# First attention: the transposes of a unit in two groups instead of four, with their splits behind one another

## The chip, the cores and the metric

The kernel runs on one core of a Trainium2 chip. The metric is the device time of one execution in microseconds (us), lower is better; it is measured as a median over runs. The core's engines work side by side and meet by semaphores: TensorE (PE in the profile, its weight loads PEld), VectorE (DVE), ScalarE (ACT), GpSimd (POOL) and SyncE (SP), which issues the transfers.

## The reference, cut to what matters

The whole program is a network of two layers, each with an attention and a block of experts. The change is in the attention of the first layer:

```python
hidden_states = concatenate([context, latents], axis=1)
q = (latents @ Wq)          # 4 batches, 256 queries, 32 heads of 128
k = (hidden_states @ Wk)    # 1857 keys, 4 key heads, each for 8 heads
v = (hidden_states @ Wv)
scores = einsum('bqhgd,bkhd->bhgqk', q, k) / sqrt(128)
attn = softmax(scores, axis=-1)
out = einsum('bhgqk,bkhd->bqhgd', attn, v)
```

Everything is float32. The kernel multiplies in a faster 32-bit form (fp32r) three times, with every operand split into a high part and a low rest: high by high, high by low, low by high.

## The kernel before, in words

`grouped_attention_block` (line 489) works through 128 units, one for each batch and head. A unit has 256 queries, as two blocks j of 128, and 1857 keys. Its work on each engine:

- **Scores** (`scores`, lines 726 to 739), on TensorE: for each j two halves of the keys. Half 0 is 1024 keys (six matmuls of 512 columns), half 1 is 833 (three of 512 columns, three of 322). They go into four PSUM banks `ps_s`, two for a half. The same four banks serve j = 0, j = 1 and the next unit, so each half waits until the exponential that read the half before it is done.
- **Maximum and negation** (`maximum`, line 872, `negate_maximum`, line 879), on VectorE: one maximum for each half as soon as it is there, then the negated maximum of both.
- **Exponentials** (`exponentials`, line 827), on ScalarE: one for each half, from PSUM into `probs` in SBUF, with the sum read out behind it (a row of its own, ACTIVATION_READ_ACCUMULATOR). Half 0 waits for the negated maximum.
- The first 1024 keys of the probabilities are turned by transfers (`trade`) and by VectorE (`turn_traded`, line 898), split by ScalarE (`turned_high`, line 836) and GpSimd (line 707), and multiplied by the values (`weigh_turned`, four groups of six matmuls).
- The other 833 keys, seven blocks, are turned by **TensorE transposes** (`turn_plain`, line 752) in four groups e = 0 to 3: four transposes each for e = 0, 1, 2 and two for e = 3. The groups go into the two banks of `ps_x` by turns (e even, e odd). `plain_high` on ScalarE (line 845) copies the high part out of the bank, `plain_low` on VectorE (line 908) takes the rest, and after it the bank is free for the group after the next. `weigh_plain` multiplies by the values: six matmuls for e = 0, 1, 2, three for e = 3.
- `take_output` (line 917) copies the unit's 256 columns out; SyncE stores them.

The three matmuls of a product stand in the helper `three` (lines 722 to 724), so a matmul's line in the profile does not tell which group it is; its tiles and its shape do.

Each engine runs its instructions in the order in which its own `step` issues them, written out by hand; a wait holds up all that stands behind it on that engine. A step of TensorE mixes four units: v (scores), w, l and z (one, two and three units further back). Batch 0 is unrolled (32 steps), the other three batches run in a loop whose body has 32 steps, and a few steps follow to drain. In the loop the semaphore counts are register values.

Short names used below: S00, S01, S10, S11 are the scores of block j and half; E00 to E11 their exponentials; m00 to m11 their maxima; T0 to T3 the groups of transposes e; ph0 to ph3 and pl0 to pl3 their high and low splits; z, l in front of T or P the groups of `weigh_turned` and `weigh_plain` of units z and l (zT2, lP0). The order on TensorE before:

zT2, zP2, T1, zP3, S00, T2, S01, zT3, T3, lT0, lP0, lT1, S10, T0, S11, lP1

On ScalarE: E10, ph1, E11, turned_high 0 and 1, ph2, E00, ph3, E01, turned_high 2 and 3, ph0. On VectorE: pl1, turn_traded 1, m00, m01, negation, turn_traded 2, take_output, pl2, turn_traded 3, m10, pl3, m11, negation, pl0, turn_traded 0.

The waits that matter: S00 needs E10 of the unit before done, S01 its E11; S10 needs E00 and S11 E01 of its own unit. ph e needs T e done; pl e needs ph e. T2 needs pl0, T3 needs pl1, T0 of the next unit needs pl2.

Of the kernel before, what the change touches and what calls it, by code (L numbers as in the profile page):

```python
# [488 lines left out]
def grouped_attention_block(nc, held, x, ctx_in, wq, wk, wv, wo, x_res, xn, stats, ident, ones):  # L489
# [40 lines left out]
    with ExitStack() as ctx:  # L530
# [16 lines left out]
        with ExitStack() as stack:  # L547
# [64 lines left out]
            def wait(engine, done, count):  # L612

                if not isinstance(count, int) or count > 0:
                    engine.wait_ge(done, count)
# [104 lines left out]
            def _(pe):  # L720
# [73 lines left out]
                def step(b, r):  # L794
                    v, w, l, z = Unit(b, r - 1), Unit(b, r - 2), Unit(b, r - 3), Unit(b, r - 4)
                    weigh_turned(z, 2)
                    weigh_plain(z, 2)
                    turn_plain(l, 1)
                    weigh_plain(z, 3)
                    scores(v, 0, 0)  # L800
                    turn_plain(l, 2)
                    scores(v, 0, 1)
                    weigh_turned(z, 3, last=True)
                    turn_plain(l, 3)
                    weigh_turned(l, 0, first=True)
                    weigh_plain(l, 0)
                    weigh_turned(l, 1)
                    scores(v, 1, 0)
                    turn_plain(w, 0)
                    scores(v, 1, 1)  # L810
                    weigh_plain(l, 1)
                    if isinstance(b, int) and b * HEADS + r == UNITS + 1:
                        turn_sums()

                run(pe, step, 4)

            @block.scalar
            def _(act):
                def exponentials(u, j, half):
                    if not u.live:  # L820
                        return
                    act.wait_ge(neg_max_done, QT * u.n + j + 1)
                    if half == 0:
                        wait(act, trade_done[j][u.a], TRADE * u.use)
                        wait(act, x_ps, PPAIRS * (u.n - 1))
                    lo, hi = HALVES[half]
                    act.activation(probs[j][u.a][:, lo:hi], s_flat[:, lo:hi], ACT.Exp, bias=neg_max[:, j:j + 1], scale=SCALE,  # L827
                                   accum_out=half_sum[:, bass.ds(QT * u.n + j, 1), half]).then_inc(probs_done, 1)

                def turned_high(u, p):  # L830
                    if not u.live:
                        return
                    q, slot = TPAIRS * u.n + p, (TPAIRS * u.r + p) % RING
                    act.wait_ge(turn_done, q + 1)
                    wait(act, tv_ps, q + 1 - RING)
                    act.activation(t_hi[:, slot, :, :], turned[:, slot, :, :], ACT.Copy).then_inc(t_hi_done, 1)  # L836

                def plain_high(u, e):
                    if not u.live:
                        return  # L840
                    q, slot, bank = PPAIRS * u.n + e, (PPAIRS * u.r + e) % PRING, (PPAIRS * u.r + e) % XBANKS
                    m, rows = len(pair_tiles(e)), plain_rows(2 * e)
                    act.wait_ge(x_ps, q + 1)
                    wait(act, xv_ps, q + 1 - PRING)
                    act.activation(x_hi[0:rows, slot, 0:m, :], ps_x[0:rows, bank, 0:TOK * m].rearrange("p (m n) -> p m n", m=m), ACT.Copy  # L845
                                   ).then_inc(x_hi_done, 1)

                def step(b, r):
                    u, v, w = Unit(b, r), Unit(b, r - 1), Unit(b, r - 2)
                    exponentials(v, 1, 0)  # L850
                    plain_high(w, 1)
                    exponentials(v, 1, 1)
                    turned_high(w, 0)
                    turned_high(w, 1)
                    plain_high(w, 2)
                    exponentials(u, 0, 0)
                    plain_high(w, 3)
                    exponentials(u, 0, 1)
                    turned_high(w, 2)
                    turned_high(w, 3)  # L860
                    plain_high(v, 0)

                run(act, step, 4)

            @block.vector
            def _(dve):
                def maximum(u, j, half):
                    if not u.live:
                        return
                    lo, hi = HALVES[half]  # L870
                    dve.wait_ge(s_ps, 4 * u.n + 2 * j + half + 1)
                    dve.reduce_max(half_max[:, half:half + 1], s_flat[:, lo:hi], AX.X).then_inc(max_done, 1)  # L872

                def negate_maximum(u, j):
                    if not u.live:
                        return
                    dve.wait_ge(max_done, 4 * u.n + 2 * j + 2)
                    wait(dve, probs_done, 4 * u.n + 2 * j - 2)
                    dve.tensor_scalar(neg_max[:, j:j + 1], half_max[:, 0:1], half_max[:, 1:2], -SCALE, ALU.max,  # L879
                                      ALU.mult).then_inc(neg_max_done, 1)  # L880

                def sums():
                    dve.wait_ge(probs_done, 4 * UNITS)
                    dve.tensor_tensor(row_sum[:, :], half_sum[:, :, 0], half_sum[:, :, 1], ALU.add).then_inc(sum_done, 1)

                def inverse_sums():
                    dve.wait_ge(sum_ps, 1)
                    dve.reciprocal(row_inv[:, :], ps_s[:, 0, 0:UNITS * QT]).then_inc(inv_done, 1)

                def turn_traded(u, p):  # L890
                    if not u.live:
                        return
                    q, slot = TPAIRS * u.n + p, (TPAIRS * u.r + p) % RING
                    if p == 0:
                        for j in range(QT):
                            dve.wait_ge(trade_done[j][u.a], TRADE * (u.use + 1))
                    wait(dve, t_done, q + 1 - RING)
                    dve.transpose(turned[:, slot, :, :].rearrange("p k (q r) -> p k q r", r=SQ),  # L898
                                  traded[:, u.a, :, :, 2 * SQ * p:2 * SQ * (p + 1)].rearrange("p j g (k r) -> p k (j g) r", k=2)
                                  ).then_inc(turn_done, 1)  # L900

                def plain_low(u, e):
                    if not u.live:
                        return
                    q, slot, bank = PPAIRS * u.n + e, (PPAIRS * u.r + e) % PRING, (PPAIRS * u.r + e) % XBANKS
                    m, rows = len(pair_tiles(e)), plain_rows(2 * e)
                    dve.wait_ge(x_hi_done, q + 1)
                    dve.tensor_tensor(x_lo[0:rows, slot, 0:m, :], ps_x[0:rows, bank, 0:TOK * m].rearrange("p (m n) -> p m n", m=m),  # L908
                                      x_hi[0:rows, slot, 0:m, :].bitcast(F32), ALU.subtract).then_inc(x_done, 1)

                def take_output(u):
                    if not u.live:
                        return
                    dve.wait_ge(tv_ps, TPAIRS * (u.n + 1))
                    dve.wait_ge(xv_ps, PPAIRS * (u.n + 1))
                    wait(dve, o_stored[u.a], 16 * u.use)
                    dve.tensor_copy(o_part[:, u.a, :], ps_o[:, u.a, 0:TOK]).then_inc(copy_done, 1)

                def step(b, r):
                    v, w, l, z = Unit(b, r - 1), Unit(b, r - 2), Unit(b, r - 3), Unit(b, r - 4)  # L920
                    plain_low(l, 1)
                    turn_traded(l, 1)
                    maximum(v, 0, 0)
                    maximum(v, 0, 1)
                    negate_maximum(v, 0)
                    turn_traded(l, 2)
                    take_output(z)
                    plain_low(l, 2)
                    turn_traded(l, 3)
                    maximum(v, 1, 0)  # L930
                    plain_low(l, 3)
                    maximum(v, 1, 1)
                    negate_maximum(v, 1)
                    plain_low(w, 0)
                    turn_traded(w, 0)
                    if isinstance(b, int) and b * HEADS + r == UNITS + 1:
                        sums()
                        inverse_sums()

                run(dve, step, 4)  # L940
# [1669 lines left out]
```

## Time and profile before

| | us |
|---|---|
| median of 3 runs | 3225.57 (3225.3 to 3226.3) |
| the profiled execution's own time | 3227.55 |
| its span, first to last instruction | 3225.8 |
| TensorE busy | 3023.2 (94%) |
| VectorE busy | 2093.0 (65%) |
| ScalarE busy | 1738.8 (54%) |
| GpSimd busy | 963.1 (30%) |

The profile is of one execution. A timeline row gives the start and length of an instruction (or of several of one kind in a row, with their count), its engine and line, and what it writes and reads; in brackets stands how long the engine was idle before it and what ended that. TensorE's matmuls are pipelined: the next starts before the length of the last is over, so the distance between starts is what one costs. Busy time counts the modelled lengths.

### The profile page before, as it was taken

Reading aid. Unit: us, or ns where it says so; the run is one execution under the profiler, and the core shown is the slowest. Engines: PE = TensorE matmul, PEld = TensorE weight load, DVE = VectorE, ACT = ScalarE, POOL = GpSimd, SP = SyncE. Lnnn points to the kernel's source line nnn. Section 1 sums busy time; section 2 is a strip of 40 time slices with the busy share of each in tenths; the row PEclk is TensorE's granted clock in tenths of the full one; section 3 lists DMA queues with packets and bytes.
Section 4 is the critical chain, followed back from the end, with each engine's and each line's share of the span. In section 5 each row is a group of like instructions: output and inputs, shape, how many; then the busy total and the mean of one; then the engine's idle time right before and its main releaser. Section 6 shows DMA issues by size and latency. Waiting matters only on the chain. (4 is left out here: it accounts for less than half of the span.)

```text
span 3225.8 us, 53851 instructions
## 1 busy us (share of the span) xinstructions
PE 3023.2 (94%) x18414; PEld 2684.3 (83%) x18414; DVE 2093.0 (65%) x3215; ACT 1738.8 (54%) x3297; POOL 963.1 (30%) x773
## 2 busy tenths in 40 slices
PE   8999998999999999999999999979889798898974
PEld 8888886899999999899998999968668788786763
DVE  4333343788888888788887888844444477665575
ACT  3323343676666666666666666632344455553263
POOL 0000121344444444444443444422100124430144
PEclk9999999999999999999999999999899799998997
DMA  7665685766767776677776676567475211101387
GB/s 250 219 217 193 218 284 191 152 161 162 162 157 161 161 161 158 157 158 162 157 160 156 157 164 152 120 189 241 138 277 166 86 29 41 41 28 33 111 294 250
DMA packets 395364, 522.17 MB, mean 162 GB/s; under 512 B 35356, under 2 KB 292684, under 8 KB 395112
## 3 DMA queue, kind: packets, MB, share of 16 engines
q1 hardware_dynamic: 392552, 510.57, 57.9%
q0 software_dynamic: 2560, 8.39, 0.8%
q8 instruction: 140, 2.29, 0.3%
q14 instruction: 112, 0.92, 0.1%
HBM read 238.15 MB, written 146.46 MB: 119 GB/s over the span
## 5 line engine op out<-in xcount | busy, mean ns | idle before, releaser
L707 POOL TENSOR_TENSOR a_t_lo<-a_turned,a_t_hi 128x512 fp32r<-128x512 f32 x512 | 649.4, 1290 | 939.5 <-ACT a_t_hi L836 939.5
L827 ACT ACTIVATE a_probs<-a_ps_s,a_neg_max 128x1024 f32<-128x1024 f32 (+1 forms) x512 | 529.6, 1034 | 475.3 <-DVE a_neg_max L879 472.5
L872 DVE TENSOR_REDUCE a_half_max<-a_ps_s 128x1 f32<-128x1024 f32 (+1 forms) x512 | 571.1, 1115 | 189.4 <-PE a_ps_s L724 185.2
L722 PE MATMUL a_ps_s<-a_k_buf,a_q_buf 128*128 128x512 f32 (+1 forms) x1024 | 419.9, 410 | 17.9 <-ACT a_probs L827 11.6
L723 PE MATMUL a_ps_s<-a_k_buf,a_q_buf 128*128 128x512 f32 (+1 forms) x1024 | 386.0, 377 | 0.0
L724 PE MATMUL a_ps_s<-a_k_buf,a_q_buf 128*128 128x512 f32 (+1 forms) x1024 | 385.2, 376 | 0.0
L908 DVE TENSOR_TENSOR a_x_lo<-a_ps_x,a_x_hi 128x512 fp32r<-128x512 f32 (+1 forms) x512 | 314.4, 614 | 107.4 <-ACT a_x_hi L845 107.4
L454 DVE TENSOR_TENSOR p_out<-p_ps_j,p_out 128x512 fp32r<-128x512 f32 (+3 forms) x196 | 152.9, 780 | 326.9 <-ACT p_out L383 326.9
L898 DVE STREAM_TRANSPOSE a_turned<-xn 128x512 f32<-128x512 f32 x512 | 357.7, 699 | 1.5 <-POOL a_t_lo L707 1.5
L383 ACT ACTIVATE p_out<-p_ps_j 128x512 fp32r<-128x512 f32 (+3 forms) x196 | 142.1, 725 | 339.5 <-PE p_ps_j L288 339.5
L722 PE MATMUL a_ps_o<-a_t_hi,a_v_buf 128*128 128x256 f32 x1024 | 298.9, 292 | 6.3 <-issue 3.8
L836 ACT ACTIVATE a_t_hi<-a_turned 128x512 fp32r<-128x512 f32 x512 | 298.4, 629 | 2.0 <-DVE a_turned L898 2.0
L845 ACT ACTIVATE a_x_hi<-a_ps_x 128x512 fp32r<-128x512 f32 (+1 forms) x512 | 274.5, 537 | 24.6 <-PE a_ps_x L752 13.0
L723 PE MATMUL a_ps_o<-a_t_lo,a_v_buf 128*128 128x256 f32 x1024 | 287.4, 281 | 0.0
L724 PE MATMUL a_ps_o<-a_t_hi,a_v_buf 128*128 128x256 f32 x1024 | 287.3, 281 | 0.0
L752 PE MATMUL a_ps_x<-a_turn,a_probs 128*128 128x128 f32 (+1 forms) x1792 | 279.1, 272 | 0.0
L722 PE MATMUL a_ps_o<-a_x_hi,a_v_buf 128*128 128x256 f32 (+1 forms) x896 | 262.3, 293 | 0.0
L724 PE MATMUL a_ps_o<-a_x_hi,a_v_buf 128*128 128x256 f32 (+1 forms) x896 | 251.6, 281 | 0.0
L723 PE MATMUL a_ps_o<-a_x_lo,a_v_buf 128*128 128x256 f32 (+1 forms) x896 | 251.3, 281 | 0.0
L752 PEld LDWEIGHTS a_ps_x<-a_turn,a_probs 128*128 128x128 f32 (+1 forms) x1792 | 219.0, 140 | 34.9 <-issue 0.2
L722 PEld LDWEIGHTS a_ps_s<-a_k_buf,a_q_buf 128*128 128x128 f32 x1024 | 195.0, 190 | 49.2 <-issue 11.7
L724 PEld LDWEIGHTS a_ps_s<-a_k_buf,a_q_buf 128*128 128x128 f32 x1024 | 194.5, 190 | 34.2
(373 smaller groups left out, 7094.6 us busy)
## 6 DMA issues: line engine op xcount, KB each, us to landing
xn<-a_probs SPq DMA_DIRECT2D x1024, 128.0 KB, 3.4
a_q_all<-p_out SPq DMA_DIRECT2D x64, 512.0 KB
a_q_buf<-a_q_all SPq DMA_DIRECT2D x128, 256.0 KB, 3.3
a_k_buf<-a_k_all SPq DMA_DIRECT2D x64, 464.5 KB, 4.0
a_v_all<-p_out SPq DMA_DIRECT2D x56, 512.0 KB
d_w_raw<-e_wt_all SPq DMA_DIRECT2D x31, 768.0 KB, 6.2
a_k_all<-p_out SPq DMA_DIRECT2D x48, 384.0 KB
a_v_buf<-a_v_all SPq DMA_DIRECT2D x64, 256.0 KB
```

The costliest lines, as they stand in the source:

```text
L454: dve.tensor_tensor(job_views(n, 1)[0], ps, hi.bitcast(F32), ALU.subtract).then_inc(job_done, 1)
L707: pool.tensor_tensor(t_lo[:, slot, :, :], turned[:, slot, :, :], t_hi[:, slot, :, :].bitcast(F32), ALU.subtract).then_inc(t_done, 1)
L722: pe.matmul(o, w_hi, m_hi, start=first, stop=False)
L723: pe.matmul(o, w_hi, m_lo, start=False, stop=False)
L724: return pe.matmul(o, w_lo, m_hi, start=False, stop=last)
L752: tr = pe.transpose(ps_x[0:rows, bank, col:col + P], probs[j][u.a][:, c0:c0 + rows], turn[:, :])
L827: act.activation(probs[j][u.a][:, lo:hi], s_flat[:, lo:hi], ACT.Exp, bias=neg_max[:, j:j + 1], scale=SCALE, accum_out=half_sum[:, bass.ds( ...
L836: act.activation(t_hi[:, slot, :, :], turned[:, slot, :, :], ACT.Copy).then_inc(t_hi_done, 1)
L845: act.activation(x_hi[0:rows, slot, 0:m, :], ps_x[0:rows, bank, 0:TOK * m].rearrange("p (m n) -> p m n", m=m), ACT.Copy).then_inc(x_hi_don ...
L872: dve.reduce_max(half_max[:, half:half + 1], s_flat[:, lo:hi], AX.X).then_inc(max_done, 1)
L898: dve.transpose(turned[:, slot, :, :].rearrange("p k (q r) -> p k q r", r=SQ), traded[:, u.a, :, :, 2 * SQ * p:2 * SQ * (p + 1)].rearrange ...
L908: dve.tensor_tensor(x_lo[0:rows, slot, 0:m, :], ps_x[0:rows, bank, 0:TOK * m].rearrange("p (m n) -> p m n", m=m), x_hi[0:rows, slot, 0:m, ...
```

## The change

Only the order in which three engines issue their instructions is changed. On TensorE T2 moves from between S00 and S01 to directly behind T1, and T0 (of the unit after) from between S10 and S11 to directly behind T3: the four groups of transposes of a step become two, T1 with T2 and T3 with T0. On ScalarE ph2 moves ahead of E11, directly behind ph1, and ph0 ahead of turned_high 2 and 3. On VectorE pl2 moves directly behind pl1. SyncE and GpSimd keep their order; no instruction is added, removed or resized.

```diff
--- before.py
+++ after.py
@@ -796,17 +796,17 @@
                     weigh_turned(z, 2)
                     weigh_plain(z, 2)
                     turn_plain(l, 1)
+                    turn_plain(l, 2)
                     weigh_plain(z, 3)
                     scores(v, 0, 0)
-                    turn_plain(l, 2)
                     scores(v, 0, 1)
                     weigh_turned(z, 3, last=True)
                     turn_plain(l, 3)
+                    turn_plain(w, 0)
                     weigh_turned(l, 0, first=True)
                     weigh_plain(l, 0)
                     weigh_turned(l, 1)
                     scores(v, 1, 0)
-                    turn_plain(w, 0)
                     scores(v, 1, 1)
                     weigh_plain(l, 1)
                     if isinstance(b, int) and b * HEADS + r == UNITS + 1:
@@ -849,16 +849,16 @@
                     u, v, w = Unit(b, r), Unit(b, r - 1), Unit(b, r - 2)
                     exponentials(v, 1, 0)
                     plain_high(w, 1)
+                    plain_high(w, 2)
                     exponentials(v, 1, 1)
                     turned_high(w, 0)
                     turned_high(w, 1)
-                    plain_high(w, 2)
                     exponentials(u, 0, 0)
                     plain_high(w, 3)
                     exponentials(u, 0, 1)
+                    plain_high(v, 0)
                     turned_high(w, 2)
                     turned_high(w, 3)
-                    plain_high(v, 0)
 
                 run(act, step, 4)
 
@@ -919,13 +919,13 @@
                 def step(b, r):
                     v, w, l, z = Unit(b, r - 1), Unit(b, r - 2), Unit(b, r - 3), Unit(b, r - 4)
                     plain_low(l, 1)
+                    plain_low(l, 2)
                     turn_traded(l, 1)
                     maximum(v, 0, 0)
                     maximum(v, 0, 1)
                     negate_maximum(v, 0)
                     turn_traded(l, 2)
                     take_output(z)
-                    plain_low(l, 2)
                     turn_traded(l, 3)
                     maximum(v, 1, 0)
                     plain_low(l, 3)
```

## Rows read from the trace of the kernel before

**Rows 1.** The page, part 1: TensorE, busy us (share of the span) and instructions
```profile
PE 3023.2 (94%) x18414; PEld 2684.3 (83%) x18414; DVE 2093.0 (65%) x3215; ACT 1738.8 (54%) x3297; POOL 963.1 (30%) x773
```

**Rows 2.** Busy time by stretch: us, then each engine's busy us (instructions), clock, DMA
```profile
540.00:560.00 20.00, 10.53 (x28) 8.09 (x29) 5.37 (x7) 5.57 (x9) 0.00 (x0) 0.71 0.32 88
600.00:929.00 329.00, 329.00 (x2289) 304.58 (x2288) 270.08 (x414) 229.32 (x440) 140.36 (x112) 1.00 0.72 161
929.00:1290.00 361.00, 360.92 (x2476) 332.34 (x2476) 292.30 (x448) 248.84 (x478) 150.11 (x119) 1.00 0.71 160
1290.00:1340.00 50.00, 47.41 (x328) 43.47 (x327) 38.60 (x60) 31.88 (x62) 20.31 (x16) 1.00 0.65 154
```

**Rows 3.** Timeline of TensorE, one unit: start, length, engine, line, operation, tiles, count
```profile
1013.97 0.28 PE L722 MATMUL a_ps_o<-a_t_hi,a_v_buf 128*128 128x256 f32 x1
...
1015.38 0.60 PE L752 MATMUL a_ps_x<-a_turn,a_probs 128*128 128x128 f32 x4
...
1016.46 0.40 PE L723 MATMUL a_ps_s<-a_k_buf,a_q_buf 128*128 128x512 f32 x1
...
1017.64 0.60 PE L752 MATMUL a_ps_x<-a_turn,a_probs 128*128 128x128 f32 x4
1018.00 0.48 PE L722 MATMUL a_ps_s<-a_k_buf,a_q_buf 128*128 128x512 f32 x1
1018.31 0.40 PE L723 MATMUL a_ps_s<-a_k_buf,a_q_buf 128*128 128x512 f32 x1
...
1019.24 0.28 PE L722 MATMUL a_ps_o<-a_t_hi,a_v_buf 128*128 128x256 f32 x1
...
1019.96 0.38 PE L752 MATMUL a_ps_x<-a_turn,a_probs 128*65 128x128 f32 x2
...
1020.30 0.28 PE L723 MATMUL a_ps_o<-a_t_lo,a_v_buf 128*128 128x256 f32 x1
...
1022.60 0.39 PE L723 MATMUL a_ps_s<-a_k_buf,a_q_buf 128*128 128x512 f32 x1
```

**Rows 4.** Timeline of ScalarE, the same unit; in brackets idle time and its releaser
```profile
1014.87 1.12 ACT L827 ACTIVATE a_probs<-a_ps_s,a_neg_max 128x1024 f32<-128x1024 f32 x1 [1.88 <-DVE a_neg_max L879]
1015.88 0.19 ACT L827 ACTIVATION_READ_ACCUMULATOR a_probs<-a_ps_s,a_neg_max  x1
1016.09 0.60 ACT L845 ACTIVATE a_x_hi<-a_ps_x 128x512 fp32r<-128x512 f32 x1
1016.59 0.95 ACT L827 ACTIVATE a_probs<-a_ps_s,a_neg_max 128x833 f32<-128x833 f32 x1
1017.42 0.20 ACT L827 ACTIVATION_READ_ACCUMULATOR a_probs<-a_ps_s,a_neg_max  x1
...
1021.00 1.12 ACT L827 ACTIVATE a_probs<-a_ps_s,a_neg_max 128x1024 f32<-128x1024 f32 x1 [1.82 <-DVE a_neg_max L879]
...
1022.11 0.37 ACT L845 ACTIVATE a_x_hi<-a_ps_x 65x256 fp32r<-65x256 f32 x1
...
1026.95 1.12 ACT L827 ACTIVATE a_probs<-a_ps_s,a_neg_max 128x1024 f32<-128x1024 f32 x1 [1.88 <-DVE a_neg_max L879]
```

**Rows 5.** Timeline of VectorE, the same unit
```profile
1014.66 0.68 DVE L908 TENSOR_TENSOR a_x_lo<-a_ps_x,a_x_hi 128x512 fp32r<-128x512 f32 x1
...
1023.96 1.23 DVE L872 TENSOR_REDUCE a_half_max<-a_ps_s 128x1 f32<-128x1024 f32 x1 [0.67 <-PE a_ps_s L724]
1025.10 0.41 DVE L908 TENSOR_TENSOR a_x_lo<-a_ps_x,a_x_hi 65x256 fp32r<-65x256 f32 x1
1025.55 1.02 DVE L872 TENSOR_REDUCE a_half_max<-a_ps_s 128x1 f32<-128x833 f32 x1
1026.61 0.21 DVE L879 TENSOR_SCALAR a_neg_max<-a_half_max 128x1 f32<-128x1 f32 x1
```

**Rows 6.** Timeline in the unrolled batch: VectorE negation and ScalarE exponential behind it
```profile
702.69 0.21 DVE L879 TENSOR_SCALAR a_neg_max<-a_half_max 128x1 f32<-128x1 f32 x1
...
702.94 1.12 ACT L827 ACTIVATE a_probs<-a_ps_s,a_neg_max 128x1024 f32<-128x1024 f32 x1 [1.84 <-DVE a_neg_max L879]
```

## The prediction, made before the changed kernel was run

> **What bounds the kernel now.** I read four views in this order: the busy shares of the page, busy time by stretch, the timelines of TensorE, ScalarE and VectorE over one unit, and the same link in the unrolled first batch. The page says TensorE is busy 94% of the span [rows 1]. By stretch it is busy for all of 600 to 929 us and of 929 to 1290 us [rows 2]; but a matmul's length in this profile is modelled, so a full row does not show that nothing waits. Count units instead. A unit has 83 matmuls (24 of scores, 24 of weigh_turned, 21 of weigh_plain, 14 transposes). So 2289 matmuls in 329 us are 27.6 units of 11.93 us, and 2476 in 361 us are 29.8 units of 12.10 us [rows 2]. The first stretch is the unrolled batch 0, the second the loop over the other batches. In the loop 0.17 us a unit go somewhere.
>
> The timeline shows where [rows 3]. Score matmuls of 512 columns follow each other every 0.235 us (1016.46 to 1017.64 for five). The first of a group is best placed by the second minus 0.235: S00 really starts at 1016.225 (1016.46 less 0.235), S01 at 1018.075, S10 at 1022.365. On ScalarE, E10 runs from 1014.87 to the end of its read-out at 1016.07, and S00 starts 0.155 later [rows 3, 4]. E00 starts at 21.00; with the same 1.20 + 0.155 it frees S10 at 1022.36, which is when S10 starts. So in the loop both first halves of the scores start when the exponential that frees their banks lets them. S01 is different: E11 ends at 1017.62, could free S01 at 1017.78, and S01 starts at 1018.075, with 0.30 us to spare. That spare is there because T2 stands between S00 and S01.
>
> **TensorE: fewer borders between transposes and matmuls.** Nothing is added or removed; 14 transposes stay 14. T2 starts at 1017.64 and the second matmul of S01 at 1018.31: 0.67, less 0.235 for the first matmul, is 0.435 for four transposes and one border. T3 starts at 1019.96 and the second matmul of lT0 at 1020.30: 0.34, less 0.12 for one of six matmuls that take 0.705 (zT2 and zP2 take 1.41), is 0.22 for two transposes and one border. From the two, a transpose takes 0.108 and a border 0.005. That the first matmul behind T2 shows 0.31 to the next (1018.00 to 1018.31) instead of 0.235 is then the last transpose, not a border. Bounds for each border taken away: 0, and 0.08 if that excess were a border after all; for 2 x 125 borders at most 20 us, and only where TensorE is the bound. I take 0, as the two equations leave nothing.
>
> What the order does is move 0.435 of work from between the score halves to in front of the first ones: S00 and S10 get 0.435 more time for E10 and E00. That removes the loop's waits there, worth at most 12.10 - 11.93 = 0.17 a unit. But S01 now follows S00 after 6 x 0.235 = 1.41 instead of 1.85.
>
> **VectorE: S11 is no longer what its maximum waits for.** m10 started at 1023.96, pl3 at 1025.10, m11 at 1025.55 [rows 5]. m11 there waited for S11: it starts 0.04 after pl3's end, where a VectorE instruction that need not wait overlaps the one ahead. With T0 gone from between, S11 is ready 0.435 earlier, but m11 still stands behind m10 (1.14) and pl3. pl3 lasts 0.41; the overlap is 0.08 (m10 lasts 1.23 and pl3 starts after 1.14), so I take 0.33, with 0.45 (the distance seen) as the upper end. m11 then starts 1.47 after m10 instead of 1.59; measured against S11's end that is 0.32 later than before. E10 slips against TensorE by that much.
>
> plain_low(l,2) moved ahead of turn_traded(l,1) delays m00 by 0.6, but S01 will be late itself (below), so m01 and E00 are not held. T0, now directly behind T3, needs pl2, which now ends before the unit's maxima start, while T0 comes behind S01 and zT3.
>
> **ScalarE: the split put in front of E11.** E11 now stands behind two plain_high instead of one. A plain_high takes 0.60 and the next exponential started 0.50 after it (1016.09 to 1016.59) [rows 4]. I take 0.50 for the added one; bounds 0.50 and 0.60, the length without overlap. T2's transposes are ready for it: ph1 could start 0.71 after T1 started, so ph2 can 0.71 after T2, at 1016.53 on this unit's clock, while ScalarE gets to it at 14.87 + 0.32 + 1.11 + 0.50 = 1016.80. What is queued behind the longer way is E11, and behind E11 on TensorE S01 and all that follows.
>
> Balance at S01: 0.30 to spare, less 0.50 (ph2), less 0.32 (E10's slip), less 0.435 (T2 gone from between) and plus 0.435 (T2 now in front of S00): about -0.5. **S01 gets a new wait.**
>
> **The loop that then sets the unit.** From S01 round to the next S01:
> - TensorE S01 to S10: S01 1.16 (1018.075 to 1019.24), zT3 0.72 (to 1019.96), T3 0.22, T0 0.435, then lT0, lP0, lT1 at 0.705: 4.66 [rows 3].
> - S10 to m10: 1022.365 to 1023.96, 1.60 [rows 3, 5].
> - m10 1.14, pl3 0.33, m11 1.06 (1025.55 to 1026.61) [rows 5].
> - negation to E10: 0.34 (1026.61 to 1026.95) [rows 4, 5].
> - E10 to ph1: 1.11, as E00 to ph3 where nothing else was awaited [rows 4].
> - ph1 and ph2: 0.50 each.
> - E11 to S01: 1.03 to the end of its read-out (1016.59 to 1017.62) and 0.155: 1.19.
>
> The sum is 12.43 us in the loop. In the unrolled batch the negation reaches E10 in 0.25 instead of 0.34 [rows 6], so 12.34. TensorE alone wants 11.93, so its wait at S01 is 0.4 to 0.5 a unit. Against 12.10 and 11.93 a unit grows by 0.33 and 0.41. With 97 steady units in the loop and 28 in the unrolled batch: 32.0 + 11.5 = 43.5 us. The profiled execution took 3227.55, so 3271.0; the median of the runs shown is 1.98 below it, so **3269**.
>
> Edits that cost nothing: plain_high(v,0) ahead of turned_high(w,2) delays the pool's splits by 0.50, whose first reader is zT2; T2's bank must be free of pl0, which ended at 15.34 [rows 5], slips 0.32, and with 0.155 is out at 15.82, just when T2 comes (15.38 + 0.435). Either wait would stand ahead of S01 on TensorE and is covered by the 0.4 to 0.5 that TensorE waits there; without that cover they would cost some hundredths each. SyncE's order is untouched; its trades still follow the same exponentials. The gaps at the loop's borders (47.41 busy of 50 between 1290 and 1340 [rows 2]) I leave as they are, give or take 3 us.
>
> The bounds of the loop are 12.38 (release and pl3 each 0.03 shorter) and 12.65 (pl3 0.45, ph2 0.60): 3263 to 3296.
>
> **Rivals.**
> A: *VectorE does not hold m11* (pl3 slips in while the maximum drains, or is much shorter at the head of the queue). Then S11 frees m11 and the loop loses 0.32: 12.11 in the loop, 12.02 unrolled. That is +1 and +2.5 us: 3229. Against: pl3 is 0.41 long and in one queue with m11. 0.05.
> B: *faster*. E11 is in time after all, because the two splits overlap the exponentials or E10 starts without slip; S01 does not wait, S00 and S10 are freed by the moved transposes, and every unit takes TensorE's 11.93: 97 x 0.17 = 16 us less, 3209, or 3189 if borders cost their upper bound. It decides at S01: the loop would have to be 0.5 shorter than my sum, more than the whole added split. 0.06.
> C: *the clock*. Between 540 and 560 us TensorE waited on exponentials for about half the time (10.53 busy of 20), and the granted clock was 0.71, part of it at the lower level of 1.2 GHz; between 1290 and 1340, with 2.6 of 50 idle, it stayed at 1.00 [rows 2]. A wait of 0.5 in 12.4 us is 4% idle, like the second row. If the clock did fall as in the first, 11.93 / 0.71 = 16.8 us a unit would give some 3830. The Trainium skill (TensorE: Matmul & The Clock Gate, section "A second HAM failure mode: psum-queue depth-cycling") says that short idle gaps between groups of matmuls that cycle through PSUM banks can make the clock swing between its levels; by that rule this change would cost hundreds of microseconds. The row from 1290 to 1340 speaks against it here. 0.01.
>
> **How the numbers follow.** The forecast has 0.88, A 0.05, B 0.06, C 0.01. About 0.2% (6.5 us) is what a measurement can tell from no change. Faster 0.06 is B; same 0.05 is A; slower 0.89 the rest. The range takes the loop's bounds and goes lower by 13 us, for a slip of E10 smaller by a third than I take it (0.1 x 125), without reaching A: 3250 to 3296.
>
> **What would show it.** In the changed trace: S01's first matmul starting about 0.16 after E11's read-out, with TensorE late there in nearly every unit; S00 and S10 no longer tied to E10 and E00; pl3 to m11 at 0.33 with no wait for S11; ph1, ph2, E11 back to back; units of 12.3 to 12.4 us in both stretches. Wrong if units take 11.9 us, if S01 follows S00 after 1.41, or if eight transposes in a row take less than 0.86.

## The result, and the profile after

| | before | after |
|---|---|---|
| median of 5 runs each, us | 3225.57 (3225.21 to 3228.38) | 3260.48 (3257.21 to 3267.31) |
| ratio, 95% interval | | 1.0107 [1.0095, 1.0118] |
| the profiled execution, us | 3227.55 | 3258.77 |
| its span, us | 3225.8 | 3257.1 |

Slower, as forecast, and inside the range (3250 to 3296). The growth is 34.9 us by the medians and 31.2 between the two profiled executions, where 43.5 was forecast.

The page, part 1, of the kernel after (as [rows 1]):

```profile
PE 3047.4 (94%) x18414; PEld 2682.0 (82%) x18414; DVE 2070.0 (64%) x3215; ACT 1720.2 (53%) x3297; POOL 961.7 (30%) x773
```

Busy time by stretch of the kernel after, columns as in [rows 2]:

```profile
600.00:929.00 329.00, 327.25 (x2227) 296.76 (x2227) 257.75 (x403) 218.77 (x429) 136.81 (x108) 1.00 0.70 158
929.00:1290.00 361.00, 357.53 (x2423) 323.88 (x2422) 280.29 (x438) 239.79 (x469) 146.89 (x116) 1.00 0.68 156
1290.00:1340.00 50.00, 47.73 (x323) 42.88 (x322) 37.74 (x60) 31.34 (x61) 20.22 (x16) 1.00 0.67 147
```

The page does not show the loss: TensorE's share is 94% both times. Nor does the busy time: 327.25 of 329 is 1.75 us idle, where 62 matmuls fewer than before [rows 2] are 9 us of work. What shows it is the count. 2227 matmuls are 26.8 units of 12.26 us, 2423 are 29.2 units of 12.37, against 11.93 and 12.10. The clock in the last columns is 1.00 in all three.

Where the time stands is seen in the timeline. TensorE after, from one S01 to the next (as [rows 3]):

```profile
1416.62 0.50 PE L722 MATMUL a_ps_s<-a_k_buf,a_q_buf 128*128 128x512 f32 x1 [0.24 <-ACT a_probs L827]
1416.96 0.40 PE L723 MATMUL a_ps_s<-a_k_buf,a_q_buf 128*128 128x512 f32 x1
...
1418.58 0.82 PE L752 MATMUL a_ps_x<-a_turn,a_probs 128*65 128x128 f32 x6
...
1419.36 0.28 PE L723 MATMUL a_ps_o<-a_t_lo,a_v_buf 128*128 128x256 f32 x1
...
1421.38 0.40 PE L722 MATMUL a_ps_s<-a_k_buf,a_q_buf 128*128 128x512 f32 x1
1421.61 0.39 PE L723 MATMUL a_ps_s<-a_k_buf,a_q_buf 128*128 128x512 f32 x1
...
1426.09 1.04 PE L752 MATMUL a_ps_x<-a_turn,a_probs 128*128 128x128 f32 x8
...
1427.09 0.28 PE L723 MATMUL a_ps_o<-a_x_lo,a_v_buf 65*128 65x256 f32 x1
...
1427.56 0.40 PE L723 MATMUL a_ps_s<-a_k_buf,a_q_buf 128*128 128x512 f32 x1
...
1428.50 0.39 PE L724 MATMUL a_ps_s<-a_k_buf,a_q_buf 128*128 128x512 f32 x1
1429.00 0.50 PE L722 MATMUL a_ps_s<-a_k_buf,a_q_buf 128*128 128x512 f32 x1
1429.34 0.40 PE L723 MATMUL a_ps_s<-a_k_buf,a_q_buf 128*128 128x512 f32 x1
```

ScalarE of the kernel after, behind the same unit's maxima (as [rows 4]):

```profile
1425.83 1.11 ACT L827 ACTIVATE a_probs<-a_ps_s,a_neg_max 128x1024 f32<-128x1024 f32 x1 [2.18 <-DVE a_neg_max L879]
...
1426.94 1.08 ACT L845 ACTIVATE a_x_hi<-a_ps_x 128x512 fp32r<-128x512 f32 x2
1427.89 0.97 ACT L827 ACTIVATE a_probs<-a_ps_s,a_neg_max 128x833 f32<-128x833 f32 x1
1428.73 0.22 ACT L827 ACTIVATION_READ_ACCUMULATOR a_probs<-a_ps_s,a_neg_max  x1
```

VectorE of the kernel after (as [rows 5]):

```profile
1422.98 1.22 DVE L872 TENSOR_REDUCE a_half_max<-a_ps_s 128x1 f32<-128x1024 f32 x1 [2.00 <-PE a_ps_s L724]
1424.12 0.41 DVE L908 TENSOR_TENSOR a_x_lo<-a_ps_x,a_x_hi 65x256 fp32r<-65x256 f32 x1
1424.45 1.01 DVE L872 TENSOR_REDUCE a_half_max<-a_ps_s 128x1 f32<-128x833 f32 x1
1425.49 0.21 DVE L879 TENSOR_SCALAR a_neg_max<-a_half_max 128x1 f32<-128x1 f32 x1
```

Read it round. S01 starts at 1416.725 (1416.96 less 0.235), S10 at 1421.375, straight behind the work in front of it. m10 starts at 1422.98, pl3 at 1424.12, m11 at 1424.45 with no wait for S11, the negation at 1425.49, E10 at 1425.83, the two splits at 1426.94, E11 at 1427.89; its read-out ends at 1428.95 and the next S01 starts 0.155 behind it, at 1429.105. That is 12.38 us, and in none of its steps is anything outside this chain waited for. S00 began at 1427.325, its six matmuls were through at 1428.735: TensorE stood 0.37 us at S01. Over the whole trace it stands there in every unit, by 0.33 in the unrolled batch and 0.38 in the loop (medians).

The waits of TensorE in the kernel after, between 590 and 2110 us (engine, line, awaited: us, times, longest):

```profile
PE a_ps_s L722 <- ACT a_probs L827: 4.0, 20, 0.3
```

4.0 us in 20 waits, where some 46 were stood through in 125 (28 x 0.33 and 97 x 0.38). A score matmul has a modelled length of 0.40 and is followed after 0.235, so the first 0.16 of a gap behind it counts as work, and a short rest is often not listed: the second S01 of TensorE's fence has no bracket though it waited 0.37.

### The profile page after: what moved, and what is told of

It reads as the page before. It is cut to its first block and busy times, and to the rows that moved or that the text cites. A ratio compares the mean times of both kernels' runs of the same rounds, so it can differ in the third digit from the quotient of the medians.

```text
span 3257.1 us, 53851 instructions
## 1 busy us (share of the span) xinstructions
PE 3047.4 (94%) x18414; PEld 2682.0 (82%) x18414; DVE 2070.0 (64%) x3215; ACT 1720.2 (53%) x3297; POOL 961.7 (30%) x773
## 5 line engine op out<-in xcount | busy, mean ns | idle before, releaser
L872 DVE TENSOR_REDUCE a_half_max<-a_ps_s 128x1 f32<-128x1024 f32 (+1 forms) x512 | 557.7, 1108 | 267.5 <-PE a_ps_s L724 267.5
L722 PE MATMUL a_ps_s<-a_k_buf,a_q_buf 128*128 128x512 f32 (+1 forms) x1024 | 399.1, 390 | 26.3 <-ACT a_probs L827 11.5
L723 PE MATMUL a_ps_s<-a_k_buf,a_q_buf 128*128 128x512 f32 (+1 forms) x1024 | 386.8, 378 | 0.0
L724 PE MATMUL a_ps_s<-a_k_buf,a_q_buf 128*128 128x512 f32 (+1 forms) x1024 | 386.4, 377 | 0.0
L908 DVE TENSOR_TENSOR a_x_lo<-a_ps_x,a_x_hi 128x512 fp32r<-128x512 f32 (+1 forms) x512 | 304.5, 616 | 86.8 <-ACT a_x_hi L845 86.8
L836 ACT ACTIVATE a_t_hi<-a_turned 128x512 fp32r<-128x512 f32 x512 | 310.8, 635 | 5.4 <-DVE a_turned L898 1.3
L722 PEld LDWEIGHTS a_ps_s<-a_k_buf,a_q_buf 128*128 128x128 f32 x1024 | 195.5, 191 | 111.4 <-ACT a_probs L827 72.5
L845 ACT ACTIVATE a_x_hi<-a_ps_x 128x512 fp32r<-128x512 f32 (+1 forms) x512 | 260.5, 535 | 10.0 <-PE a_ps_x L752 7.2
L752 PE MATMUL a_ps_x<-a_turn,a_probs 128*128 128x128 f32 (+1 forms) x1792 | 237.8, 273 | 1.9 <-DVE a_x_lo L908 1.5
L724 PEld LDWEIGHTS a_ps_s<-a_k_buf,a_q_buf 128*128 128x128 f32 x1024 | 195.1, 190 | 33.9
L723 PEld LDWEIGHTS a_ps_s<-a_k_buf,a_q_buf 128*128 128x128 f32 x1024 | 195.1, 191 | 28.7
```

Source lines behind the costliest of these rows:

```text
L722: pe.matmul(o, w_hi, m_hi, start=first, stop=False)
L723: pe.matmul(o, w_hi, m_lo, start=False, stop=False)
L724: return pe.matmul(o, w_lo, m_hi, start=False, stop=last)
L752: tr = pe.transpose(ps_x[0:rows, bank, col:col + P], probs[j][u.a][:, c0:c0 + rows], turn[:, :])
```

## The experiments

The theory: ph2 ahead of E11 and pl3 ahead of m11 stand in a loop E10, ph1, ph2, E11, S01, S10, m10, pl3, m11, negation, E10, which is longer than TensorE's own work. The rivals: the borders between transposes and matmuls, the other moved splits (pl2, ph0), VectorE's order. Units below are worked out as in the prediction: the length of the stretch, by its matmuls, times 83. Each ratio is to the kernel before, run beside that kernel.

| run | ratio to before, 95% | unit 600 to 929 | unit 990 to 1290 |
|---|---|---|---|
| before | 1 | 11.93 (x2289) | 12.09 (x2059) |
| after | 1.0107 [1.0095, 1.0118] | 12.26 (x2227) | 12.36 (x2015) |
| e9, changed kernel again | 1.0095 [1.0079, 1.0110] | 12.27 (x2226) | 12.41 (x2007) |
| e1, pl3 later | 1.0055 [1.0042, 1.0068] | 12.08 (x2260) | 12.27 (x2029) |
| e2, ph2 behind E11 | 1.0061 [1.0048, 1.0074] | 11.92 (x2291) | 12.31 (x2023) |
| e3, splits and T0 later | 0.9939 [0.9926, 0.9952] | 11.92 (x2290) | 11.95 (x2083) |
| e4, first pair only | 1.0107 [1.0093, 1.0121] | 12.10 (x2257) | 12.38 (x2011) |
| e5, before, pl3 later | 0.9996 [0.9985, 1.0006] | 11.93 (x2289) | 12.08 (x2062) |
| e6, e3 with a border | 0.9936 [0.9922, 0.9950] | 11.92 (x2291) | 11.93 (x2088) |
| e8, e3, TensorE as before | 0.9999 [0.9990, 1.0008] | 11.93 (x2289) | 12.09 (x2060) |
| e10, e3, ph2 ahead | 1.0110 [1.0094, 1.0125] | 12.24 (x2231) | 12.42 (x2005) |
| e11, e10, pl3 later | 1.0055 [1.0041, 1.0069] | 12.10 (x2257) | 12.21 (x2039) |

**e1: pl3 out of the loop.** The changed kernel with

```diff
                     maximum(v, 1, 0)
-                    plain_low(l, 3)
                     maximum(v, 1, 1)
                     negate_maximum(v, 1)
+                    plain_low(l, 3)
                     plain_low(w, 0)
```

> The changed kernel with one line moved on VectorE: the small split pl3 goes from between the two maxima m10 and m11 to behind the negation. Theory (the loop S01, S10, m10, pl3, m11, E10, ph1, ph2, E11, S01 sets the unit): pl3's 0.33 us leaves the loop, m11 starts as soon as S11 is ready. The loop alone would then take 12.04 us, but ph1 is next held by T1: S01 to S10 4.64, S10 and S11 2.54, lP1, zT2, zP2 2.14, T1 to its release 0.61, ph1 0.06 behind it, ph1 and ph2 0.95, E11 to S01 1.21, together 12.16. So 12.16 us a unit instead of 12.37 in the loop and 12.28 in the unrolled batch: 97 x 0.21 + 28 x 0.12 = 24 us less than the changed kernel, about 3236. Rival 1 (only ScalarE's split ahead of E11 matters, VectorE has room): no change, 3260. Rival 2 (the eight transposes in a row cost TensorE time themselves): no change, 3260.

3247.34 us, less than the changed kernel but 11 more than expected: the unrolled batch came out shorter by 0.18 a unit (0.12 expected), the loop by only 0.09 (0.21 expected). With E10 earlier the loop meets the next thing, the transposes. The timeline of TensorE in e1 has T1 and T2 at:

```profile
1442.10 1.04 PE L752 MATMUL a_ps_x<-a_turn,a_probs 128*128 128x128 f32 x8
```

The timeline of ScalarE in e1, E10 and the two splits behind it:

```profile
1441.48 1.12 ACT L827 ACTIVATE a_probs<-a_ps_s,a_neg_max 128x1024 f32<-128x1024 f32 x1 [1.82 <-DVE a_neg_max L879]
...
1442.81 1.09 ACT L845 ACTIVATE a_x_hi<-a_ps_x 128x512 fp32r<-128x512 f32 x2
```

ph1 starts 1.33 behind E10, not 1.11, and 0.71 behind T1's start: it waits for T1. So pl3 is one term of the loop, and taking it away is worth less than its 0.33 because T1 is late next.

**e2: ph2 out of the loop.** The changed kernel with

```diff
                     plain_high(w, 1)
-                    plain_high(w, 2)
                     exponentials(v, 1, 1)
+                    plain_high(w, 2)
                     turned_high(w, 0)
...
                     exponentials(u, 0, 1)
-                    plain_high(v, 0)
                     turned_high(w, 2)
                     turned_high(w, 3)
+                    plain_high(v, 0)
...
                     plain_low(l, 1)
-                    plain_low(l, 2)
                     turn_traded(l, 1)
+                    plain_low(l, 2)
                     maximum(v, 0, 0)
```

> The changed kernel with TensorE's order kept (two groups of transposes), but ScalarE's ph2 behind E11 instead of ahead of it, ph0 behind the turned splits as before the change, and VectorE's pl2 behind turn_traded 1. Theory: E11 is freed 0.48 us earlier and S01 no longer waits. The next loop runs through pl2, which now holds the maximum m00: S10 to E10 4.46, E10, ph1, E11 2.51, ph2 and pl2 1.23, m00, m01 2.16, negation to E00 0.50, E00 to S10 1.36: 12.21 us in the loop, and less than TensorE's own 11.95 in the unrolled batch. So S10 waits for E00 in the loop, S01 for nothing: 97 x 0.16 + 28 x 0.33 = 25 us less than the changed kernel, about 3235. Rival 2 (eight transposes in a row cost TensorE time): S01 and S10 wait for nothing and the time stays at 3260.

3248.40 us. S01 no longer waits and the unrolled batch is back at TensorE's 11.92. But the loop stayed at 12.31, where 12.21 was expected, with another wait, at S10. The timeline of VectorE in e2 (pl2, m00 with m01, negation):

```profile
1440.81 0.69 DVE L908 TENSOR_TENSOR a_x_lo<-a_ps_x,a_x_hi 128x512 fp32r<-128x512 f32 x1
1441.41 2.15 DVE L872 TENSOR_REDUCE a_half_max<-a_ps_s 128x1 f32<-128x1024 f32 x2
1443.69 0.21 DVE L879 TENSOR_SCALAR a_neg_max<-a_half_max 128x1 f32<-128x1 f32 x1
```

The timeline of ScalarE in e2 (ph2, then E00 and its read-out):

```profile
1440.17 0.60 ACT L845 ACTIVATE a_x_hi<-a_ps_x 128x512 fp32r<-128x512 f32 x1
...
1444.10 1.12 ACT L827 ACTIVATE a_probs<-a_ps_s,a_neg_max 128x1024 f32<-128x1024 f32 x1 [2.29 <-DVE a_neg_max L879]
1445.12 0.19 ACT L827 ACTIVATION_READ_ACCUMULATOR a_probs<-a_ps_s,a_neg_max  x1
```

The timeline of TensorE in e2, the first two matmuls of S10:

```profile
1445.36 0.50 PE L722 MATMUL a_ps_s<-a_k_buf,a_q_buf 128*128 128x512 f32 x1
1445.70 0.39 PE L723 MATMUL a_ps_s<-a_k_buf,a_q_buf 128*128 128x512 f32 x1
```

pl2 starts 0.64 behind ph2, the maxima stand behind pl2, E00 behind their negation, and S10 starts at 1445.465, 0.155 behind E00's read-out. From the first maximum to the negation it takes 2.28, where the expectation had 2.16: that is the 0.1. A split that nothing needs soon, placed ahead of the maxima, closes the next loop.

**e3: the pairs of transposes kept, the splits where nothing waits.** The changed kernel with

```diff
                     turn_plain(l, 3)
-                    turn_plain(w, 0)
                     weigh_turned(l, 0, first=True)
                     weigh_plain(l, 0)
+                    turn_plain(w, 0)
                     weigh_turned(l, 1)
...
-                    plain_high(w, 2)
                     exponentials(v, 1, 1)
                     turned_high(w, 0)
+                    plain_high(w, 2)
                     turned_high(w, 1)
...
-                    plain_high(v, 0)
                     turned_high(w, 2)
                     turned_high(w, 3)
+                    plain_high(v, 0)
...
                     plain_low(l, 1)
-                    plain_low(l, 2)
                     turn_traded(l, 1)
...
                     negate_maximum(v, 0)
+                    plain_low(l, 2)
                     turn_traded(l, 2)
```

T1 and T2 stay a pair and the score halves stay unbroken; T0 no longer stands beside T3.

> T1 and T2 stay together ahead of S00 and both pairs of score groups stay together, but the splits are put where nothing waits for them: ph2 behind turned_high 0, pl2 behind the first negation, ph0 behind the turned splits, and T0 behind lP0 (it needs pl2). Theory: no loop through the exponentials is longer than TensorE's own work, so every unit takes TensorE's 11.95 us in both stretches: 97 x 0.42 + 28 x 0.33 = 50 us less than the changed kernel and 14 less than the kernel before: about 3211. Rival 2 (the transposes together cost TensorE time): no better than 3245. A rival that VectorE or GpSimd are late elsewhere (turned splits for zT2): 3225 to 3240, with the wait at zT2 or lT0.

3209.41 us, faster than both kernels: 0.9939 [0.9926, 0.9952]. Busy time by stretch of e3:

```profile
600.00:929.00 329.00, 329.00 (x2290) 307.38 (x2290) 268.15 (x416) 222.10 (x440) 140.11 (x111) 1.00 0.73 161
990.00:1290.00 300.00, 299.94 (x2083) 279.20 (x2082) 244.24 (x377) 203.28 (x402) 126.91 (x100) 1.00 0.73 162
```

The timeline of ScalarE in e3 (ph1, E11, its read-out, turned_high 0, ph2):

```profile
1410.51 0.59 ACT L845 ACTIVATE a_x_hi<-a_ps_x 128x512 fp32r<-128x512 f32 x1
1410.98 0.96 ACT L827 ACTIVATE a_probs<-a_ps_s,a_neg_max 128x833 f32<-128x833 f32 x1
1411.82 0.21 ACT L827 ACTIVATION_READ_ACCUMULATOR a_probs<-a_ps_s,a_neg_max  x1
1411.91 0.64 ACT L836 ACTIVATE a_t_hi<-a_turned 128x512 fp32r<-128x512 f32 x1
1412.43 0.60 ACT L845 ACTIVATE a_x_hi<-a_ps_x 128x512 fp32r<-128x512 f32 x1
```

The timeline of TensorE in e3, the first matmuls of S00 and S01:

```profile
1410.85 0.39 PE L722 MATMUL a_ps_s<-a_k_buf,a_q_buf 128*128 128x512 f32 x1
...
1412.26 0.39 PE L722 MATMUL a_ps_s<-a_k_buf,a_q_buf 128*128 128x512 f32 x1
```

S01 follows S00 after 1.41 us, six matmuls and nothing else. E11's read-out ends at 1412.03, so with 0.155 the banks were free at 1412.185, 0.07 in time. This is what rival B of the prediction described and gave at 3209; it needed another order of splits.

**e4: only the first pair of the change.** The changed kernel with T0 and ph0 where they were before:

```diff
                     turn_plain(l, 3)
-                    turn_plain(w, 0)
...
                     scores(v, 1, 0)
+                    turn_plain(w, 0)
                     scores(v, 1, 1)
...
-                    plain_high(v, 0)
                     turned_high(w, 2)
                     turned_high(w, 3)
+                    plain_high(v, 0)
```

> Half of the change: T2 with T1 on TensorE, ph2 behind ph1, pl2 behind pl1, while T0 and ph0 stay where they were before the change (T0 between S10 and S11). Theory: with T0 between them m11 waits for S11 again and pl3 is hidden, but ph2 still stands ahead of E11: the loop through T1, ph1, ph2, E11 takes 12.16 us (S01 to S10 4.21, S10, T0, S11 2.98, lP1, zT2, zP2 2.14, T1 and ph1 0.67, ph1, ph2 0.95, E11 to S01 1.21), and S10 waits some 0.08 for E00: 12.24 in the loop, 12.16 unrolled. Against the kernel before: 97 x 0.14 + 28 x 0.22 = 20 us more, about 3245, 15 less than the whole change. Rival 1 (ph2 ahead of E11 is the whole cost, the second pair costs nothing): 3260, as the whole change. Rival 2 (each pair of groups costs TensorE the same): half of 35, 3243, but with no wait at S01.

3259.51 us: the first pair alone costs as much as the whole change, which the expectation missed. The timeline of VectorE in e4 (m10, pl3, m11):

```profile
1418.27 1.23 DVE L872 TENSOR_REDUCE a_half_max<-a_ps_s 128x1 f32<-128x1024 f32 x1 [1.71 <-PE a_ps_s L724]
1419.41 0.41 DVE L908 TENSOR_TENSOR a_x_lo<-a_ps_x,a_x_hi 65x256 fp32r<-65x256 f32 x1
1419.86 1.03 DVE L872 TENSOR_REDUCE a_half_max<-a_ps_s 128x1 f32<-128x833 f32 x1
```

The timeline of TensorE in e4 (S10's second matmul, T0, then T1 with T2):

```profile
1416.90 0.40 PE L723 MATMUL a_ps_s<-a_k_buf,a_q_buf 128*128 128x512 f32 x1
...
1418.07 0.60 PE L752 MATMUL a_ps_x<-a_turn,a_probs 128*128 128x128 f32 x4
...
1421.77 1.03 PE L752 MATMUL a_ps_x<-a_turn,a_probs 128*128 128x128 f32 x8
```

The timeline of ScalarE in e4, E10 and the two splits behind it:

```profile
1421.26 1.12 ACT L827 ACTIVATE a_probs<-a_ps_s,a_neg_max 128x1024 f32<-128x1024 f32 x1 [1.88 <-DVE a_neg_max L879]
...
1422.48 1.09 ACT L845 ACTIVATE a_x_hi<-a_ps_x 128x512 fp32r<-128x512 f32 x2
```

With T0 between S10 and S11, m11 follows m10 after 1.59, as before [rows 5], not after 1.47: it waits for S11, and pl3 hides in that wait. But m11 is not what the unit waits for: ph1 starts 1.22 behind E10, not 1.11, and 0.71 behind T1's start, so it is T1 that holds ph1, as in e1. TensorE then waits at S01 for E11 (0.18 in the unrolled batch, 0.26 in the loop, by the medians). In the loop it also waits at S10, here at 1416.665, for E00 (0.17; the expectation had 0.08), and E00 stands behind ph2 and pl2. The medians of the loop, round from S10: to T1 5.12, to ph1 0.715, to ph2 0.49, to pl2 0.74, to m00 1.22, to the negation 2.24, to E00 0.50, to S10 1.36, together 12.385, the unit. In the unrolled batch, where S10 has no such wait, the unit is 12.10 (12.16 expected). So the first pair alone closes a loop of its own, through T1, ph2 and pl2 and not through m11; that it takes the same time as the whole change, as the expectation's first rival had it, is chance: the units of the two stretches differ.

**e5: pl3 alone, in the kernel before.** The edit of e1, made in the kernel before.

> The kernel before with only pl3 moved on VectorE, from between m10 and m11 to behind the negation. Theory (pl3 costs only where S10 and S11 follow each other, since m11 otherwise waits for S11): no change, units of 11.94 and 12.10 us, S11 still ending the wait of m11. Rival (the split between the maxima always delays the exponential): a third of a microsecond off the way from S10 to E10, so S00 no longer waits, 97 x 0.04 = 4 us less; not more, since S10's wait on E00 stays.

3227.46 us, 0.9996 [0.9985, 1.0006]. Before the change pl3 was hidden; the change uncovered it, as the prediction had it.

**e6: the border by itself.** e3 with T2 one group further back:

```diff
                     turn_plain(l, 1)
-                    turn_plain(l, 2)
                     weigh_plain(z, 3)
+                    turn_plain(l, 2)
                     scores(v, 0, 0)
```

> The kernel in which TensorE was the bound (splits later), with T2 behind zP3 instead of directly behind T1: one border between transposes and matmuls more in each unit, all else the same. Theory (a border costs some 0.005 us): units stay at 11.94 to 11.95, the time within 1 us or so of that kernel. Rival (the 0.08 us that the first matmul behind a group of transposes shows is a border's cost): 125 x 0.08 = 10 us more, units of 12.03.

3210.36 us, 0.9936 against e3's 0.9939. Borders cost nothing that can be measured, so pairing the transposes has no gain of its own.

**e8: e3's splits with TensorE's order of before.**

```diff
                     turn_plain(l, 1)
-                    turn_plain(l, 2)
                     weigh_plain(z, 3)
                     scores(v, 0, 0)
+                    turn_plain(l, 2)
                     scores(v, 0, 1)
...
                     weigh_plain(l, 0)
-                    turn_plain(w, 0)
                     weigh_turned(l, 1)
                     scores(v, 1, 0)
+                    turn_plain(w, 0)
                     scores(v, 1, 1)
```

> The same places of the splits on ScalarE and VectorE as in the kernel in which TensorE was the bound, but TensorE's order of the kernel before (four groups of transposes, T2 and T0 between the halves of the scores). Theory (the gain of that kernel comes from the transposes moved out from between the halves, which give E10 and E00 0.435 us more): as the kernel before, units of 11.94 and 12.10, S10 and S00 waiting on their exponentials in the loop. Rival (the gain comes from the later splits): 11.95 in both stretches, some 15 us less than before.

3228.46 us, 0.9999 [0.9990, 1.0008], with the units of before. So e3's gain comes from where the transposes stand: ahead of the score halves that used to wait, where they fill 0.17 us a unit of the loop.

**e9: the changed kernel again**, beside the three above.

> The changed kernel once more, so that it stands beside the others on one chip: 31 to 38 us over the kernel before, units of 12.28 and 12.37 us, S01 waiting 0.33 and 0.39.

3262.36 us. Between chips and runs the result holds.

**e10: one line of the change put into e3.**

```diff
                     plain_high(w, 1)
+                    plain_high(w, 2)
                     exponentials(v, 1, 1)
                     turned_high(w, 0)
-                    plain_high(w, 2)
                     turned_high(w, 1)
```

> The kernel in which TensorE was the bound (splits later) with one line moved on ScalarE: ph2 from behind turned_high 0 to directly behind ph1, ahead of E11, as the change has it. Theory (that place alone closes the loop): units of 12.28 us in the unrolled batch and 12.37 in the loop as in the changed kernel, against 11.94 and 11.95: 28 x 0.34 + 97 x 0.42 = 50 us more, about 3260, with S01 the only group that waits. Rival (the cost of the change is the sum of several edits: pl2, ph0, T0 too): about half of that.

3262.87 us: 1.0110 where e3 has 0.9939, 53 us between the medians (55 by the ratios). The timeline of ScalarE in e10, E11 and its read-out:

```profile
1413.27 0.95 ACT L827 ACTIVATE a_probs<-a_ps_s,a_neg_max 128x833 f32<-128x833 f32 x1
1414.10 0.20 ACT L827 ACTIVATION_READ_ACCUMULATOR a_probs<-a_ps_s,a_neg_max  x1
```

The timeline of TensorE in e10, the first two matmuls of S01:

```profile
1414.36 0.50 PE L722 MATMUL a_ps_s<-a_k_buf,a_q_buf 128*128 128x512 f32 x1 [0.24 <-ACT a_probs L827]
1414.70 0.40 PE L723 MATMUL a_ps_s<-a_k_buf,a_q_buf 128*128 128x512 f32 x1
```

S01 starts at 1414.465, 0.165 behind E11's read-out, as after the change, and no other group of TensorE waits. pl2, ph0 and T0 stand elsewhere than in the changed kernel and the time is the same: with S00 and S01 unbroken, ph2 ahead of E11 alone decides.

**e11: e10 with pl3 later** (the edit of e1 on top).

> The same with pl3 behind the second negation. Theory (pl3 is in the loop only through m11, then T1 holds ph1; with ph0 back behind the turned splits zT2 no longer waits 0.055 as it did when pl3 was moved in the changed kernel): 12.12 us unrolled and 12.26 - 0.055 = 12.21 in the loop, so 28 x 0.16 + 97 x 0.16 = 20 us less than with ph2 ahead alone, about 3240. Rival (pl3 does not matter): 3260. Rival (zT2's wait was no part of that loop): 12.26, 3245.

3244.45 us, 18 less than e10. pl3 is about a third of the 53. The loop's unit, 12.21, is also shorter than e1's 12.27. e1 has ph0 ahead of turned_high 2 and 3 and a wait of 0.055 at zT2, e11 has neither; that fits with that wait being a part of e1's loop, though pl2 and T0 differ as well.

## Why the prediction was right

- **S01 gets a new wait: right.** The balance of about -0.5 read 0.37 in the unit shown; its sign and its place held, and e10 and e3 show that ph2 sets it.
- **The loop, term by term** (forecast, then the unit shown): S01 to S10 4.66, 4.65; S10 to m10 1.60, 1.605; m10 1.14, 1.14; pl3 0.33, 0.33; m11 1.06, 1.04; negation to E10 0.34, 0.34; E10 to ph1 1.11, 1.11; the two splits 1.00, 0.95; E11 to S01 1.19, 1.215. Sum 12.43, measured 12.38. The mis-sized terms are ph1 and ph2, 0.477 each by the median over the trace, where the distance of 0.50 had been read from one that an exponential followed [rows 4], and m11, 1.046, where 1.06 had been read from one that had waited for its scores [rows 5].
- **The sum.** Medians over the units, from S01 to S01, are 12.28 unrolled and 12.37 in the loop, against 11.94 and 12.11 in the kernel before: 28 x 0.34 + 97 x 0.26 = 34.7 us. From the first unit's S01 to the last one's the profiled executions took 1541.97 and 1576.86 us, 34.9 more. So all of the 8.6 us between 43.5 and 34.9 is in the units: 0.06 in each of those after (the splits and m11), 0.01 in each of those before.
- **The range held in part by luck.** 3260.48 lies below the loop's own bounds (3263 to 3296), in the part added for a slip of E10 smaller than forecast. That slip came as forecast (m11 1.47 behind m10); it was the splits and m11 that were shorter.
- **pl3 uncovered: right** (rival A fell). m11 starts 0.33 behind pl3; e5 shows the cover of before, e1 and e11 the price without it. Rival A's price would not have held: with pl3 out of the way (e1) T1 holds ph1, and the loop's unit is 12.27, not 12.11, the time 3247, not 3229.
- **Rival B fell for this change**: E11 was late by what ph2 adds. Its price held, in e3.
- **Rival C fell**: with TensorE waiting at S01 in every unit the granted clock was 1.00 in all stretches of the attention shown above. The Trainium skill (TensorE: Matmul & The Clock Gate, section "A second HAM failure mode: psum-queue depth-cycling") warns of short gaps between groups that cycle through PSUM banks; gaps of 0.37 in 12.4 us moved no clock here.
- **Borders at nothing: right.** Eight transposes took 0.88 (1426.09 to 1427.09, less 0.12 for one matmul), six 0.66 (1418.58 to 1419.36, less 0.12): 0.11 each, as 0.108 was worked out; e6 confirms it by time.
- **Edits at nothing: right, by their cover.** zT2 did wait in the loop, 0.05 by the median, and TensorE would have stood that much longer at S01. The delay of m00 by pl2 does reach m01 and E00, which the prediction had as not held, but by little: m01 starts 1.393 behind S01, in e10, without that delay, 1.347 (medians of the loop), and S10 has 0.27 to spare.

## What to carry to other kernels

Before moving an instruction on an in-order engine, read the slack of the wait behind it: S01 had 0.30 us, and one split of 0.48 ahead of the exponential that frees its banks closed a loop over three engines. Nearly the same move of the transposes, without that split, gains 0.6% (e3), so cost each queue's edit by itself and put what nothing needs soon behind what frees a bank. Count the work done in a stretch (here matmuls) rather than busy time or listed waits, since modelled lengths cover short gaps.

## What the runs showed that was not expected

- Two maxima back to back and the negation behind them take, in e2, 2.28 us from the start of the first in the loop (1441.41 to 1443.69) and 2.18 in the unrolled batch (694.29 to 696.47). The negation also reaches E10 in 0.34 in the loop and 0.25 unrolled [rows 4 to 6]. The loop differs by semaphore counts held in registers; that this is the cause was not tried.
- Splits of 0.59 us follow each other after 0.477 on ScalarE.
- Five runs say little about spread: those of the changed kernel lie within 10 us and those of the kernel before within 3, but 21 runs of the kernel before, taken beside e5, lie within 13 (3220.60 to 3233.39).
